# Attention block on one core: the last head group's pair sums, its last tiles' x, and the final normalisation

## The reference, cut to what matters

```python
att = softmax(where(causal, q @ k.T / sqrt(32), -1e9))      # per head
y = att @ v                                                 # all heads side by side
x = x + ga * (y @ W_proj + b_proj)
h = layernorm(x) * (1 + cb) + sb
x = x + gb * (layernorm(h) * ln_g + ln_b)                   # what the kernel writes out
```

## Time and profile before

| | |
|---|---|
| three runs, median | 3232.7 us |
| the profiled execution, its own time | 3227.0 us |
| span of that profile | 3225.2 us |
| granted PE clock, mean over the span | 0.971 |
| PE busy | 2992.1 us (93%) |
| DVE, ACT, POOL busy | 2489.4, 1842.8, 1589.7 us |
| the last group's first score product starts | 3024.90 us |
| the last step's PE products end | 3179.72 us |
| DVE starts the end's reciprocals | 3185.68 us |

### The profile page before, as it was taken

The page is one execution under the profiler, slowest core; times in us unless marked ns, Lnnn a source line. Parts: engine busy times, 40 slices in busy tenths (PEclk is TensorE's granted clock), DMA queues, the critical chain, the costliest instruction groups (busy, mean ns, idle before and its releaser), DMA issues.

```text
span 3225.2 us, 59202 instructions
## 1 busy us (share of the span) xinstructions
PE 2992.1 (93%) x21664; PEld 1164.8 (36%) x21664; DVE 2489.4 (77%) x4206; ACT 1842.8 (57%) x3659; POOL 1589.7 (49%) x1602
## 2 busy tenths in 40 slices
PE   4899999999999999999999999999999999999886
PEld 1334444335343433434333243433324343242222
DVE  4787777777778788777878878777887878878477
ACT  4316665886655555785555555587545555454541
POOL 3204343572626365482645727365472646637355
PEclk7869999999999999999999999999999999999997
DMA  6302121313041310413123041311314122031121
GB/s 239 84 20 58 28 64 24 94 37 77 14 107 40 78 53 24 103 40 87 40 65 85 27 97 34 87 50 40 87 35 118 40 65 58 32 72 45 57 78 64
DMA packets 181932, 205.28 MB, mean 64 GB/s; under 512 B 21492, under 2 KB 137460, under 8 KB 180996
## 3 DMA queue, kind: packets, MB, share of 16 engines
q1 hardware_dynamic: 181640, 201.50, 23.9%
HBM read 114.09 MB, written 36.50 MB: 47 GB/s over the span
## 4 chain that ended last, share of the span: by engine, by line
PE 41%; issue 19%; DVE 14%; POOL 11%; POOLq 7%; ACT 3%; DVEq 3%; DMA 2%; ACTq 1%; SPq 0%
DVE mpart L965 9%; PE ps_out L1287 8%; PE ring L1237 8%; PE ps_scores L1273 6%; PE ps_scores L1211 5%; POOL psum L564 5%; PE ps_den L1304 4%; POOL psum L563 3%; PE ps_den L1310 3%; PE ring L1259 3%; PE ps_scores L1223 2%; POOLq L599 2%; POOLq L535 1%; POOLq L591 1%; ACT prob L788 1%
## 5 line engine op out<-in xcount | busy, mean ns | idle before, releaser
L788 ACT ACTIVATE prob<-ps_scores 128x512 f32<-128x512 f32 (+3 forms) x2560 | 1248.2, 537 | 949.9 <-PE ps_scores L1276 460.8
L965 DVE TENSOR_REDUCE mpart<-ring 128x1 f32<-128x512 f32 (+3 forms) x2560 | 1401.1, 599 | 347.5 <-PE ring L1237 185.3
L1237 PE MATMUL ring<-qk 96*128 96x512 f16 (+3 forms) x2560 | 873.5, 363 | 68.1 <-DVE mpart L965 48.8
L1273 PE MATMUL ps_scores<-qk 98*128 98x512 f16 (+3 forms) x2560 | 862.5, 350 | 35.7 <-ACT prob L788 28.9
L563 POOL TENSOR_TENSOR psum<-prob 128x512 f32<-128x512 f32 x360 | 480.7, 1335 | 376.8 <-ACT prob L788 302.0
L1287 PE MATMUL ps_out<-prob,v 128*32 128x512 f32 (+3 forms) x5120 | 602.4, 543 | 0.0
L1237 PEld LDWEIGHTS ring<-qk 96*128 96x128 f16 x2560 | 234.5, 98 | 815.8 <-DVE mpart L965 538.8
L564 POOL TENSOR_TENSOR psum<-prob 128x512 f32<-128x512 f32 x360 | 480.0, 1333 | 0.0
L1273 PEld LDWEIGHTS ps_scores<-qk 98*128 98x128 f16 x2560 | 246.0, 98 | 360.2 <-ACT prob L788 216.5
L1211 PE MATMUL ps_scores<-hT,wg 128*128 128x512 f16 x1536 | 346.2, 382 | 5.8 <-POOL hT L554 5.8
L582 POOL TENSOR_TENSOR xs<-xs,bc 128x512 f32<-128x512 f32 x60 | 81.1, 1351 | 426.1 <-DMA xs<-in_L_attn_x_dram 425.1
(11 more groups left out here) (129 smaller groups left out, 2605.0 us busy)
## 6 DMA issues: line engine op xcount, KB each, us to landing
turn<-in_rope_dram SPq DMA_DIRECT2D x64, 512.0 KB, 4.6
xs<-in_L_attn_x_dram SPq DMA_DIRECT2D x108, 256.0 KB, 2.8
qk<-prob SPq DMA_DIRECT2D x192, 128.0 KB, 3.7
qk<-half SPq DMA_DIRECT2D x192, 128.0 KB, 3.7
attn_out_T<-ot SPq DMA_DIRECT2D x63, 256.0 KB, 2.1
otin<-attn_out_T SPq DMA_DIRECT2D x30, 512.0 KB, 4.6
out_dram<-x SPq DMA_DIRECT2D x60, 256.0 KB, 2.1
wg<-w_qkv_halves SPq DMA_DIRECT2D x16, 768.0 KB, 5.5
```

The lines of the kernel that those rows point to most:

```text
L788: act.activation(prob[:, s % 3, p, h % 2, 0:w], ps_scores[(HG * s + h) % NBK][:, 0:w], ACT.Exp, scale=SCALE).then_inc(exp_done, 1)
L965: dve.tensor_reduce(mpart[:, h, qt, kc:kc + 1], ring[use % NBK][:, 0:w], AX.X, ALU.max).then_inc(ring_free, 1)
L1237: mm = pe.matmul(ring[use % NBK][:, 0:w], qk[0:R, G % 2, 0, h, qt * P:(qt + 1) * P], qk[0:R, G % 2, 1, h, kc * QC:kc * QC + w], start=True ...
L1273: mm = pe.matmul(ps_scores[k % NBK][:, 0:w], qk[0:RM, par, 1, h, kt * P:(kt + 1) * P], qk[0:RM, par, 0, h, cq * QC + q0:(cq + 1) * QC], st ...
```

## The change

1. Pair sums are made in the last group too: POOL gets 12 `add_pair` (48 additions), PE loses the 24 separate denominator products of whole steps and gets 12 products with the sums, and ACT's exponentials of the steps s+3 and s+4 wait for the pair at s.
2. Since `psum2` is no longer free, the x of tiles 12 to 15 goes into the operand tile `qk` of the other parity, which the last group doesn't read. SP issues these four loads at the group's start instead of at step 38, and POOL adds the bias row to one of them in each of the steps 32, 34, 36 and 38 instead of in a row after the last step.
3. At the end DVE only makes the reciprocals and the products; ACT makes the 16-bit copies and POOL the remainders.
4. DVE's `tail_third` of tile 11 moves from step 39 to behind the end's reciprocals and products.

```diff
@@ tail_buffers
-                return end_x[:, i, :], end_wk[:, i, :], end_x1[:, i, :]
+                return last_x[:, i, :], end_wk[:, i, :], end_x1[:, i, :]
@@ SP, the last group, ahead of its steps
+                    if own:
+                        sp.wait_ge(scores_done, HG * NS * (NG * B - 1))
+                        for t in range(NT - TPC, NT):
+                            sp.dma_start(last_x[:, t - (NT - TPC), :], x[B - 1, t * P:(t + 1) * P, :]).then_inc(last_x_ld, 16)
@@ SP, step 38
-                            sp.wait_ge(pair_used, NP * (NG * B - 1))
-                            sp.wait_ge(tail_x_bias, NT * B - TPC)
-                            for t in range(NT - TPC, NT):
-                                load_x(B - 1, t, end_x[:, t - (NT - TPC), :])
                             end_attention(NT - TPC)
@@ POOL, step loop
-                        if s - 1 in PAIRS and nxt:
+                        if s - 1 in PAIRS:
                             add_pair(G, PAIRS.index(s - 1))
...
+                        if s - 1 in own and own[s - 1] >= 2 * TPC:
+                            i = own[s - 1] - 2 * TPC
+                            pool.wait_ge(last_x_ld, 16 * TPC)
+                            pool.tensor_tensor(last_x[:, i, :], last_x[:, i, :], bc[:, 1, :], ALU.add).then_inc(last_x_bias, 1)
@@ POOL, after the steps
-            for t in range(NT - TPC, NT):
-
-                tail_x(B - 1, t, NT * (B - 1) + (NT - 2 + t % 2) // 2)
+            for part in range(TPC):
+                cols = slice(part * P, (part + 1) * P)
+                pool.wait_ge(end_high, part + 1)
+                pool.tensor_tensor(ot16[:, 1, cols], osum[:, cols], ot16[:, 0, cols], ALU.subtract).then_inc(end_split, 1)
@@ ACT, exponentials
-                            elif nxt and (s - 3 in PAIRS or s - 4 in PAIRS):
+                            elif s - 3 in PAIRS or s - 4 in PAIRS:
@@ ACT, after the steps
+            for part in range(TPC):
+                cols = slice(part * P, (part + 1) * P)
+                act.wait_ge(end_normed, part + 1)
+                act.copy(ot16[:, 0, cols], osum[:, cols]).then_inc(end_high, 1)
@@ DVE, step loop and end
-                        if s - 2 in own:
+                        if s - 2 in own and own[s - 2] < NT - TPC - 1:
                             tail_third(b, own[s - 2])
...
-                dve.tensor_tensor(osum[:, cols], osum[:, cols], dsum[:, cols], ALU.mult)
-                dve.drain()
-                dve.tensor_copy(ot16[:, 0, cols], osum[:, cols])
-                dve.drain()
-                dve.tensor_tensor(ot16[:, 1, cols], osum[:, cols], ot16[:, 0, cols], ALU.subtract).then_inc(end_split, 1)
+                dve.tensor_tensor(osum[:, cols], osum[:, cols], dsum[:, cols], ALU.mult).then_inc(end_normed, 1)
+            tail_third(B - 1, NT - TPC - 1)
@@ PE, values and denominators (the argument paired is gone)
-                if kt < TPC * cq and paired:
+                if kt < TPC * cq:
...
-                if kt >= TPC * cq or not paired:
+                if kt >= TPC * cq:
```

More of the change, by code:

```diff
@@ L213, in halves @@
             return spare_half if c % 2 == 0 else half
+        last_x = qk_words[:, 0:TPC * C].rearrange("p (t n) -> p t n", n=C)
         def tail_buffers(b, t):
@@ L238, in adaln_block_kernel @@
         turn_free = sem("turn_free")
-        col_ld, bc_ld, ot_dma = (sem(n) for n in ("col_ld", "bc_ld", "ot_dma"))
+        col_ld, bc_ld, ot_dma, last_x_ld, last_x_bias = (
+            sem(n) for n in ("col_ld", "bc_ld", "ot_dma", "last_x_ld", "last_x_bias"))
         x_ld, ot_ld, out_dma = ([sem(f"{n}{i}") for i in range(2)] for n in ("x_ld", "ot_ld", "out_dma"))
@@ L260, in adaln_block_kernel @@
             sem(n) for n in ("scores_done", "exp_done", "prob_used", "pair_sum", "pair_used"))
-        sums_left, recip_done, out_normed, out_hi, out_split, end_split = (
-            sem(n) for n in ("sums_left", "recip_done", "out_normed", "out_hi", "out_split", "end_split"))
+        sums_left, recip_done, out_normed, out_hi, out_split, end_split, end_normed, end_high = (
+            sem(n) for n in ("sums_left", "recip_done", "out_normed", "out_hi", "out_split", "end_split", "end_normed",
+                             "end_high"))
         tail_x_bias, tail_x1_sum, tail_stats1, tail_rstd1, tail_x1_shift, tail_stats2, tail_rstd2, tail_done = (
@@ L307, in _, with load_x @@
         def _(sp):
-            def load_x(b, t, to=None):
+            def load_x(b, t):
                 if not isinstance(b, int):
                     sp.wait_ge(mod_st, 32)
-                sp.dma_start(xs[:, t % 2, :] if to is None else to, x[b, t * P:(t + 1) * P, :]).then_inc(x_ld[t % 2], 16)
+                sp.dma_start(xs[:, t % 2, :], x[b, t * P:(t + 1) * P, :]).then_inc(x_ld[t % 2], 16)
             def load_columns(b):
@@ L845, in _ @@
             batches(body)
+            act.wait_ge(ot_dma, 16 * (NC_ * NG * B - 1))
+            for part in range(TPC):
+                cols = slice(part * P, (part + 1) * P)
+                act.wait_ge(end_normed, part + 1)
+                act.copy(ot16[:, 0, cols], osum[:, cols]).then_inc(end_high, 1)
         @block.vector
@@ L1036, in tail_first @@
                     dve.wait_ge(out_dma[i], 16 * (NT // 2 * b + t // 2))
-                dve.wait_ge(tail_x_bias, Z + 1)
+                if t < NT - TPC:
+                    dve.wait_ge(tail_x_bias, Z + 1)
+                else:
+                    dve.wait_ge(last_x_bias, t - (NT - TPC) + 1)
                 dve.tensor_tensor(wk_, ring[use % NBK][:, :], bc[:, 0, :], ALU.mult).then_inc(ring_free, 1)
@@ L1277, in scores, with values @@
                 mm.then_inc(scores_done, 1)
-            def values(G, par, s, paired):
+            def values(G, par, s):
                 cq, kt = STEPS[s]
@@ L1289, in values, with denominators @@
                                    stop=kt == TPC * (cq + 1) - 1)
-                if kt < TPC * cq and paired:
+                if kt < TPC * cq:
                     mm.then_inc(prob_used, 1)
-            def denominators(G, s, paired):
+            def denominators(G, s):
                 cq, kt = STEPS[s]
-                if s - 2 in PAIRS and paired:
+                if s - 2 in PAIRS:
                     j = PAIRS.index(s - 2)
@@ L1358, in body @@
                             if place == (3 if plain or s > 1 and STEPS[s - 1][1] == 0 else 2) and s > 0:
-                                values(G, par, s - 1, nxt)
+                                values(G, par, s - 1)
                             if place == 3 and s > 0:
-                                denominators(G, s - 1, nxt)
+                                denominators(G, s - 1)
                             if place < len(units):
```

## The result

The changed kernel takes 3265.7 us (median of 4 runs, 3263.5 to 3266.8), the kernel before 3231.9 beside it (3230.1 to 3234.5): a ratio of 1.0104 (95% 1.0088 to 1.0120), 33.8 us slower. The forecast was 3252.5 with 3244 to 3268. Its direction and its engine were right; its sum, +19.8 us, was too small by 14.

The account below looks back on a forecast made before the run. POOL's in-order queue was to become the bound, 11.5 us a tile against PE's 8.8 before. 12.8 + 5.2 + 3.3 - 1.5 = +19.8 us gave 3246.8 on the profiled execution, 3252.5 against the median, range 3244 to 3268.

Parts of the forecast that it names:

- PE bounds all three: Last group before the change, steps 12-19, 25-30, 32-39: PE sets the pace, busy 34.94 of 35.20 us in the first.
- POOL over 90% busy: Sign that the forecast is right: POOL's busy share in steps 12 to 19 of the new profile.
- (a): Last group up to step 19, until tail_x of tile 4: +12.8 us (low 10.4, high 18.4).
- the first round: POOL's queue for one of tiles 0 to 3, from pair sum to next pair sum: 11.5 us each.
- (b): Tiles 4 to 6, which meet no pair: the 8.4 us loop stays, +0.
- (c): From tail_x of tile 6 to attention block 2's store: 28.6 us instead of 23.4, +5.2 (low 4.4, high 8.5).
- (d): From tile 8's product to the end's reciprocals: 44.7 us instead of 41.4, +3.3 (low 2.1, high 8.5).
- (e): The end, from the reciprocals on: 2.5 us gained, less DVE's stand for tile 14; together -1.5 (-2.5 to -0.4).
- The stall before tile 14: At the end: DVE stands 0.4 to 2.1 us for tile 14's product, whose load comes late.
- PE's gain is what counts: Rival: POOL's additions fit into its waits and PE's saving shows; -14.0 us, 3218.7 us; chance 6%.
- The wait for tile 8 takes the delay up: Rival: block 2's out_low comes no later, only (d) and (e) count; +1.8, 3234.5 us; chance 10%.
- DVE and POOL hold each other up throughout: Rival: DVE's operations stop POOL 2.25 us a pair instead of 0.39; 16.7 us more, 3269 us; chance 8%.

Follow-up runs that it names:

- e1: Changed kernel without pair sums in the last group, the rest of the change kept; ratio 0.9974 to the kernel before.
- e7: Changed kernel, but in the last group PE forms all denominators directly and POOL's additions read old rows, nobody waiting for them; ratio 1.0074 to the kernel before.
- e5: Changed kernel without last-group pair sums, PE's off-diagonal denominator products reading only each probability's upper 16 bits; ratio 0.9980 to the kernel before.
- e6: Changed kernel, but in the last group PE forms every denominator directly; POOL's sums stay unread, exponentials still wait for them; ratio 1.0086 to the kernel before.
- e8: Changed kernel, but in the last group only the pairs of steps 4 and 6 are summed on POOL; ratio 0.9999 to the kernel before.
- e11: Changed kernel, but the last group's pairs of steps 24 and 26 are PE's direct products again; ratio 1.0082 to the kernel before.
- e12: Changed kernel, but in the last group only the pairs of steps 28, 30, 32 and 34 are summed on POOL; ratio 1.0021 to the kernel before.
- e4: Changed kernel, but the modulation's rows (tile bc) are loaded ahead of the last group's steps, not behind block 0's store; ratio 1.0087 to the kernel before.

## Why the prediction was right, and where its sum was short

**Direction and mechanism: right.** It said that POOL becomes the bound by its queue and that PE's gain lies under waits. e1 and e7 show the first (without the sums there is no loss; where nobody waits for them, at least 26.7 of the 38.4 us stay), e5 and e6 the second. Of the places that it named, e8, e11 and e12 bear out block 0's way out, the store of block 2 and tiles 8 to 11; for tiles 0 to 3 there are only the marks. Some sentences need mending. "PE bounds all three" stretches was read from its busy time, and e5 shows that it does not: 11.7 us less of PE's work moved the length by 0.4. The Trainium skill (Perfetto Trace Analysis, section Identifying the Most-Contended Engine) would have the engine with the highest occupancy optimised first, but for TensorE it says that the busy share of its matmuls is not a good measure of how near it is to its roofline. The trace agrees with that exception: PE was busy 91% of e1's stretch. And "POOL over 90% busy" in steps 12 to 19 did not come; it was 76%, with the rest in hand-overs. `tail_x` came every 11.8 to 14.6 us in place of 11 to 13, `out_low` of block 2 30.3 us later and not 15 to 20, and the reciprocals 36.5 and not 21.

**(a) +12.8 predicted, +20.7 measured** (`tail_x` of tile 4 at 3124.80 - 6.70 = 3118.10, before 3097.41). First, waits were left out ahead of the first round. Pair 6 waited 1.92 us for PE's use of pair 4's sums. Then pair 12 started at 3076.82 - 6.70 = 3070.1, not 3065.5: it waited 3.55 us for the exponentials of step 13, which stood behind tile 0's product, itself late by its load and slow. The prediction followed `tail_x` there and not the way over PE and ACT. Together that is 4.6 us. Second, the rounds measured 13.25, 14.39 and 12.34 us (3076.82, 3090.07, 3104.46, 3116.80), 40.0 in all against 34.5 + 2.4: 3.1 us. Most of it is DVE's second part: from the end of the first inverse to the second statistics it took 4.5 us in each round and not 3.65, 2.5 us in all, since both its three-input operations stood beside POOL's. The three pairs took 4.96, 6.30 and 5.82 us and not 5.34, 1.1 in all; `out_norm`, `out_low` and the gaps took 1.5 more; the inverses, at 0.84 to 0.88 us and not 1.2, gave 2.0 back.

**(b) 0 predicted, +1.6 measured**: from tile 4 to tile 6 18.47 us instead of 16.85. The loop of 8.4 us holds, with one slow first turn.

**(c) +5.2 predicted, +8.0 measured** (31.41 against 23.40). The two pairs took 6.07 and 6.31 us and not 5.3, DVE's second part behind the first of them 4.5 and not 3.65, and `tail_third` 2.3 and not 1.6. The 6.6 us from the store to tile 8's product were 6.59.

**(d) +3.3 predicted, +6.15 measured** (3181.27 to 3228.86, 47.59 against 41.44). The rounds were as I said for the first pair (11.47 us) and 12.8 for the second; the pairs 32 and 34 took 5.86 and 5.83 us. By e12 and e1 the pairs cost 7 us from tile 8's `tail_first` on, and the moved `tail_third` gives 2.6 back (34.4 in e1, 37.0 before); the other 1.7 lie ahead of that, between the product's start and `tail_first`.

**(e) -1.5 predicted, -3.4 measured.** The reciprocals to tile 12 are 6.42 us (6.95 was the sum). The stall before tile 14 did not come: its load was issued 6.9 us after the reciprocals, as predicted, PE waited 2.06 us for it, but it was there 3.8 us after its issue, not 5, and tile 14 followed tile 12 by 7.33 us, exactly as in the earlier trace rows.

Together 20.7 + 1.6 + 8.0 + 6.15 - 3.4 = 33.1. What was too small is, first, the price of DVE and POOL beside each other: the sum took 0.39 us for it on a pair, from a mean over the whole run that shows little of it, and 0.85 us on the second of DVE's operations in its high end alone. Next to it are the waits ahead of the first round, 4.6 us, which were put at nothing. That the range held is in part luck: (a) went over its own high end (18.4) and (e) under its own low one (-2.5), which offset each other in part, and 3265.7 lies 2.3 us under the range's top.

**The rivals.** "PE's gain is what counts" fell (e5, e6). "The wait for tile 8 takes the delay up" fell: tile 8's product came 30.3 us later (3181.27 - 6.70 against 3144.24). "DVE and POOL hold each other up throughout" was right in its mechanism and not in its price: seven of the twelve pairs took 5.8 to 6.3 us, 0.9 to 1.4 over the undisturbed 4.95, between the 0.39 taken and the 2.25 of that rival; the other five took 4.9 to 5.4. Its price also left out that DVE is held up in turn.

## What to carry to other kernels

An engine's free time inside a stretch is not free if the work around it is a chain through that engine's in-order queue: price an added operation by the round of that chain, with its length beside the neighbours that it will have there, and not by the busy share. Before work is moved off the busiest engine, take that work away alone (as e5 does): if the time stays, the trade has nothing to gain. And split a change that has two parts; here the part at the end gained 5.3 us and was hidden under a loss of 38.4.

## What was not expected of the hardware

DVE and POOL exclude each other, one instruction at a time. Beside pair sums an addition on POOL goes from 1.27 to a mean of 1.40 to 1.47 us and at most 1.73, and DVE's operations with two full inputs grow too. Two such lines of DVE, in e1 and in the changed kernel's last group (busy, mean ns):

```profile
L1072 DVE SCALAR_TENSOR_TENSOR wk<-wk,rstd,bc 128x512 f32<-128x512 f32 x12 | 10.7, 894 | 0.9
...
L1086 DVE SCALAR_TENSOR_TENSOR x<-wk,rstd,xs 128x512 f32<-128x512 f32 x11 | 9.0, 819 | 0.8
```

```profile
L1069 DVE SCALAR_TENSOR_TENSOR wk<-wk,rstd,bc 128x512 f32<-128x512 f32 x12 | 15.0, 1250 | 0.9
...
L1083 DVE SCALAR_TENSOR_TENSOR x<-wk,rstd,xs 128x512 f32<-128x512 f32 x11 | 13.2, 1202 | 0.8
```

The first grows by 0.36 us and the second by 0.38. How it comes about is seen in one place of the changed kernel:

```profile
3152.69 1.27 POOL L610 TENSOR_TENSOR xs<-x,bc 128x512 f32<-128x512 f32 x1
3152.76 1.75 DVE L1067 SCALAR_TENSOR_TENSOR wk<-x,mv,bc 128x512 f32<-128x512 f32 x1 [1.56 <-POOL rstd L540]
...
3153.91 1.72 POOL L586 TENSOR_TENSOR xs<-xs,bc 128x512 f32<-128x512 f32 x1
...
3154.58 1.60 DVE L1069 SCALAR_TENSOR_TENSOR wk<-wk,rstd,bc 128x512 f32<-128x512 f32 x1
```

DVE's L1067 starts 0.07 us after POOL's L610 and ends 0.55 after its end; POOL's L586, which starts while L1067 runs, ends 1.12 after L1067's end; DVE's L1069, started while L586 runs, again ends 0.55 after it. From 3071 to 3228 us 36 of DVE's operations with two full inputs in SBUF (lines 1057, 1067, 1069, 1081 and 1083) started within a POOL operation of 128 by 512, and 35 of them ended 0.54 to 0.57 us after its end, whether it had 0.2 or 1.2 us left to run. Both figures are under what the operations take alone (0.69 to 0.75 and 1.27 us), so the later one does the main part of its work only when the other has ended. An operation grows by no more than what is left of the other when it starts, and not by the other's whole length: POOL's addition by 0.46 us at most. The Trainium skill (SBUF — State Buffer, section Who interferes with whom) has two such instructions exclude each other, and the trace agrees.

How much of the 38.4 us is this contention was not tried by itself. Nor was what the fall of PE's granted clock (0.84 from the group's start on, 0.89 before the change) costs beyond the one product seen in e4. Also open is how the rest divides beyond e7's bound: at most 11.7 us through the exponentials' wait, at least 26.7 through what stands behind the additions.
